# Linear attention with a butterfly FFN on one core: k^T (x | 1) in groups of 256 features, every key bank emptied by VectorE, and the whole last batch's attention output made by tokens

## What is computed

```python
q, k, v = split(x @ W_qkv)                      # 16 heads of 64 features each
q, k = relu(q @ W_f + b_f), relu(k @ W_f + b_f) # per head
kv = einsum('bhnd,bhne->bhde', k, v)
out = einsum('bhnd,bhde->bhne', q, kv)
out = out / (einsum('bhnd,bhd->bhn', q, k.sum(axis=2))[..., None] + 1e-06)
x = layernorm(x + merge_heads(out) @ W_out + b_out)
h = butterfly(x @ W_exp + b_exp, up_weights)    # 9 stages, 512 hidden features
h = butterfly(gelu(h + up_bias), down_weights)  # 9 stages
x = layernorm(x + h @ W_con + b_con + down_bias)
```

## Time and profile before

| | |
|---|---|
| median of three runs | 328.9 us |
| the profiled execution: time, span of its instructions | 328.99 us, 327.2 us |
| PE, PEld busy (share of the span) | 95%, 72% |
| DVE, ACT, POOL busy | 76%, 48%, 30% |
| chain that ended last, by engine | PE 76%, DVE 14%, issue 4%, ACT 2%, DMA 1%, POOL 1% |
| largest lines of that chain | ring L651 28%, kx_ps L738 14%, spare_ps L841 7%, attn_ps L651 7%, ring L758 4% |
| DMA queues | 33.95 MB, mean 104 GB/s |

### The profile page before, as it was taken

One profiled execution on the slowest core, in us unless ns is written; L12 is line 12 of the kernel. 1 busy time (PEld: TensorE's weight loads), 2 busy tenths in 40 slices (PEclk: granted clock), 3 DMA queues, 4 the chain that ended last, 5 costly groups with the idle time before them and its releaser, 6 DMA issues.

```text
span 327.2 us, 5512 instructions
## 1 busy us (share of the span) xinstructions
PE 311.2 (95%) x2009; PEld 234.4 (72%) x2009; DVE 249.9 (76%) x501; ACT 156.3 (48%) x279; POOL 97.1 (30%) x83
## 2 busy tenths in 40 slices
PE   5999999999999899999999999999999799999893
PEld 4766677767766677667768777776797587669793
DVE  3579989978989779888890997579838953758844
ACT  3634436535733343654461556346647846431442
POOL 4059999970000002400210122002302312423513
PEclk9999999999999989999999999999999999999998
DMA  4993425556705700370064002900190174372001
GB/s 140 311 327 128 134 75 184 189 201 148 175 2 136 151 0 2 103 160 0 5 156 105 0 35 68 195 0 32 20 229 16 36 167 94 93 159 75 1 34 64
DMA packets 19762, 33.95 MB, mean 104 GB/s; under 512 B 3960, under 2 KB 6680, under 8 KB 19736
## 3 DMA queue, kind: packets, MB, share of 16 engines
q1 hardware_dynamic: 19432, 33.54, 38.9%
q10 hardware_dynamic: 304, 0.07, 0.1%
HBM read 31.24 MB, written 2.36 MB: 103 GB/s over the span
## 4 chain that ended last, share of the span: by engine, by line
PE 76%; DVE 14%; issue 4%; ACT 2%; DMA 1%; POOL 1%; SPq 0%; POOLq 0%; DVEq 0%; ACTq 0%
PE ring L651 28%; PE kx_ps L738 14%; PE spare_ps L841 7%; PE attn_ps L651 7%; PE ring L758 4%; PE desk L772 3%; DVE qn L1335 2%; PE desk L660 2%; PE ring L718 2%; PE desk L747 2%; DVE k_total L1301 1%; DVE qn_l L1203 1%; DVE stats L1344 1%; DMA q<-in_L_attn_W_qkv_dram 1%; DVE k L1275 1%
## 5 line engine op out<-in xcount | busy, mean ns | idle before, releaser
L599 POOL TENSOR_TENSOR rstd<-var_eps,minus_half 128x4 f32<-128x4 f32 x14 | 19.3, 1381 | 176.9 <-DVE var_eps L1350 176.9
L1029 ACT ACTIVATE q<-ring,bf_col 128x512 f32<-128x512 f32 x64 | 43.9, 685 | 46.4 <-PE ring L651 45.6
L738 PE MATMUL kx_ps<-k,xs 128*128 128x512 f32 x128 | 60.3, 594 | 0.0
L1335 DVE TENSOR_TENSOR qn<-q,recips 128x512 f32<-128x512 f32 x64 | 43.5, 719 | 2.8 <-DMA recips<-recip_rows 2.8
L1013 ACT ACTIVATE qn_h<-qn 128x512 fp32r<-128x512 f32 x48 | 29.5, 625 | 27.5 <-DVE qn L1335 27.5
L582 POOL TENSOR_TENSOR y<-hid,y_up 128x512 f32<-128x512 f32 x18 | 32.8, 1843 | 15.9 <-DMA hid<-in_L_ffn_up_weights_dram 14.9
L738 PEld LDWEIGHTS kx_ps<-k,xs 128*128 128x128 f32 x128 | 24.2, 191 | 18.0 <-issue 15.4
L1301 DVE TENSOR_TENSOR k_total<-k_total,k 128x1024 f32<-128x1024 f32 x24 | 36.5, 1520 | 0.5 <-ACT k L1020 0.3
L1203 DVE TENSOR_TENSOR qn_l<-qn,qn_h 128x512 fp32r<-128x512 f32 x48 | 33.4, 704 | 2.9 <-ACT qn_h L1013 2.7
L651 PE MATMUL ring<-xT_h,wq_h 128*128 128x512 f32 x64 | 35.6, 556 | 0.0
L1275 DVE TENSOR_TENSOR k<-ring,bf_minus 128x512 f32<-128x512 f32 x32 | 21.9, 685 | 13.7 <-PE ring L651 13.7
(11 more groups left out here) (174 smaller groups left out, 580.6 us busy)
## 6 DMA issues: line engine op xcount, KB each, us to landing
recips<-recip_rows SPq DMA_DIRECT2D x64, 256.0 KB, 5.4
hid<-in_L_ffn_up_weights_dram SPq DMA_DIRECT2D x9, 512.0 KB, 4.2
x<-_L_ffn_down_weights_dram SPq DMA_DIRECT2D x9, 512.0 KB, 6.7
out_dram<-y SPq DMA_DIRECT2D x7, 256.0 KB, 2.0
xs<-in_L_attn_x_dram SPq DMA_DIRECT2D x3, 512.0 KB, 6.1
q<-in_L_attn_W_qkv_dram SPq DMA_DIRECT2D x2, 512.0 KB, 4.5
xs<-in_L_attn_x_dram SPq DMA_DIRECT2D x2, 256.0 KB, 2.7
q<-in_L_attn_W_qkv_dram SPq DMA_DIRECT2D x2, 256.0 KB, 3.9
```

The lines of the kernel that those rows point to most:

```text
L599: g.tensor_tensor(rstd[i][:, :], var_eps[i][:, :], minus_half[:, :].to_broadcast([128, QUADS]), ALU.pow).then_inc(s_rs[i], 1)
L738: t_.matmul(kx_ps[half], xs[b % XBUF][:, t, :], k[kt % KRING][:, half * CH:(half + 1) * CH], start=t == 0, stop=t == TILES - 1).then_inc(s ...
L1029: a_.activation(q[:, i % QRING, :], bank(("q", i))[:, :], ACT.Relu, bias=bf_col[:, :])\
L1335: v.tensor_tensor(qn[:, a % NRING, :], q[:, a % QRING, :], recips[:, a % PAIRS // RC, a % RC, :], ALU.mult).then_inc(s_qn, 1)
```

## The change

- **Key tiles by features.** A key tile is now 256 features (group g of a batch) by 512 tokens (chunk c). Each half of it holds 2 token tiles of 256 features side by side in a bank, so `project_k` makes six fp32r matmuls of 256 columns where it made three of 512.
- **All keys as max(z, -b).** The bias matmul, its rows and `k_relu` are gone; `k_max` on VectorE empties all 64 halves.
- **kx turned round.** `add_kx` takes the key (128 x 128) as weights and streams x with a column of ones behind it (129 columns), eight matmuls for a key tile, into one bank for each group. The last column is the sum of the keys, so `k_sum`, `k_total` and `ksum` are gone. ScalarE copies a group out (`kx_copy`), TensorE transposes it back (`transpose_kx`, eight 128 x 128 a batch, through `desk`), `kx_end` reads that by halves, and `ksum_mask` reads the sums from SBUF. xs has rows of 129 floats, the ones are written by GpSimd.
- **The start.** The first loads are x tiles 0 and 1, 256 columns of the k weights, x tiles 2 and 3; the other folds are spread over slots 0 to 4.
- **The butterflies.** Down stage 0 lies in slots 2 to 4, stages 1 to 8 in slots 5 to 12, one a slot, in two parts; `bias_row_step` is on GpSimd; the copies of wdn and vo are ScalarE's. Loads are reordered: up stages 4 and 5 and the last two batches of x go ahead of down stage 2, up 6 to 8 ahead of down 3, and `spread(0)` ahead of down 7.
- **The last batch by tokens.** Chunk 6 is made by tokens too; VectorE adds it to x straight from PSUM at the end of slot 38 (`add_x_before_last`), and the next chunk's first step waits for that. The bias b_out is added to the whole last batch of x by GpSimd.

The core of the diff:

```diff
@@ slots and tables
-    KX_SLOT = {TILES * b + FIRST + 1: b for b in range(BATCH)}
+    KXE_SLOT = {(TILES * b + 2 * g - 1 if b else g + 2): (b, g) for b in range(BATCH) for g in range(GROUPS)}
+    KXT_SLOT = {FIRST: (0, 0), FIRST + 2: (0, 1), TILES + FIRST: (1, 0), TILES + 6: (1, 1)}
+    for b in range(2, BATCH):
+        KXT_SLOT[TILES * b + 2] = (b, 0)
+        KXT_SLOT[TILES * b + 6] = (b, 1)
...
-    DOWN_STEP_SLOT = {1: 0, 2: 1, 3: 2, 5: 3, 6: 4, 7: 5, 8: 6, 9: 7, 12: 8}
+    DOWN_STEP_SLOT = {n + 4: n for n in range(1, STAGES)}
@@ SyncE
-            load_x(0, slice(0, 1), s_xs0)
-            for half in range(2):
-                cols = slice(HD + half * CH, HD + (half + 1) * CH)
-                sp.dma_start(wqkv_raw[:, cols], W_qkv[:, cols]).then_inc(s_wk[half], 16)
-            sp.wait_ge(s_wk[1], 16)
-            load_x(0, slice(1, 2), s_xs[0])
+            sp.dma_start(xs[0][:, 0:2, 0:C], xs_view[0, :, 0, 0:2, :]).then_inc(s_xs0[0], 16)
+            load_wk(0, slice(HD, HD + 256))
+            sp.dma_start(xs[0][:, 2:4, 0:C], xs_view[0, :, 0, 2:4, :]).then_inc(s_xs0[1], 16)
+            sp.wait_ge(s_wk[0], 16)
+            load_x(0, [1], s_xs[0])
+            load_wk(1, slice(HD + 256, HD + CH))
+            load_wk(2, slice(HD + CH, HD + 2 * CH))
...
+            load_down(3)
+            load_down(4)
             load_down(5)
             load_down(6)
+            spread(0)
             load_down(7)
-            spread(0)
             load_down(8)
@@ project_k
-                split(dst, (xT_h[:, b % 2, tok], xT_l[:, b % 2, tok]), (wk_h[:, cols], wk_l[:, cols]), stop=False)
-                t_.matmul(dst, ones_r[:, :], bf_rows[:, :], start=False, stop=True).then_inc(s_made, 1)
+                cols = slice(g * 256, (g + 1) * 256)
+                for i in range(2):
+                    t = QUADS * c + 2 * half + i
+                    tok = slice(t * 128, (t + 1) * 128)
+                    last = split(bank(("k", kt, half))[:, i * 256:(i + 1) * 256],
+                                 (xT_h[:, b % 2, tok], xT_l[:, b % 2, tok]), (wk_h[:, cols], wk_l[:, cols]))
+                last.then_inc(s_made, 1)
@@ add_kx
+                if c == 0 and GROUPS * b + g >= 2:
+                    pe.wait_ge(s_kxe, GROUPS * b + g - 1)
                 emptied(pe, ("k", kt, 1))
                 for half in range(2):
-                    t_.matmul(kx_ps[half], xs[b % XBUF][:, t, :], k[kt % KRING][:, half * CH:(half + 1) * CH],
-                              start=t == 0, stop=t == TILES - 1).then_inc(s_kxt, 1)
+                    for i in range(2):
+                        for j in range(2):
+                            col = half * CH + i * 256 + j * 128
+                            last = t_.matmul(kx_ps[g % 2][:, j * C1:(j + 1) * C1], k[kt % KRING][:, col:col + 128],
+                                             xs[b % XBUF][:, QUADS * c + 2 * half + i, :],
...
+            def transpose_kx(b, half):
+                take_desk(("kxT", b, half))
+                pe.wait_ge(s_kxe, GROUPS * b + 2 * half + 2)
+                transpose_tiles(desk, lambda i: kxT_pairs[:, 4 * half + i, 0:C]).then_inc(s_dmade, 1)
@@ add_attn
-                if a >= BATCH * STEPS - PAIRS:
+                elif a == PAIRS * LAST:
+                    pe.wait_ge(s_x1before, 1)
+                if a >= WHOLE:
@@ ScalarE
+            def kx_copy(b, g):
+                act.wait_ge(s_kxt, 2 * (TILES * b + 2 * (g + 1)))
+                if b:
+                    act.wait_ge(s_dmade, desk_of["kxT", b - 1, g // 2] + 1)
+                    act.wait_ge(s_kcols, b)
+                a_.activation(kxT[:, 2 * g * C1:2 * (g + 1) * C1], kx_ps[g % 2][:, 0:2 * C1], ACT.Copy).then_inc(s_kxe, 1)
@@ VectorE
             def ksum_mask(b):
-                dve.wait_ge(s_dmade, desk_of["ksum", b] + 1)
+                dve.wait_ge(s_kxe, GROUPS * (b + 1))
+            def add_x_before_last():
+                n = LAST - 1
+                at = n % CHUNKS * QUADS
+                dve.wait_ge(s_at, PAIRS * LAST)
+                dve.wait_ge(s_pre, n - X1BUF + 1)
+                dve.wait_ge(s_xb, 1)
+                v.tensor_tensor(x1[:, n % X1BUF, :, :], attn_ps[:, :].rearrange("p (t c) -> p t c", t=QUADS),
+                                xs[(BATCH - 1) % XBUF][:, at:at + QUADS, 0:C], ALU.add).then_inc(s_x1before, 1)
```

More of the change, by code:

```diff
@@ L192, in postln_linear_attention_butterfly_ffn_kernel @@
             order.append(("x", *XT_SLOT[s]))
-        if s == WDN_SLOT:
-            order.append(("wdn",))
+        if s == FIRST:
+            order.append(("vo", 3))
         if s in X1T_SLOT:
@@ L323, in postln_linear_attention_butterfly_ffn_kernel @@
         desk = pb("desk")
[L325 removed]
+        s_wk = [sem(f"k_weights_part_{n}_loaded") for n in range(3)]
         s_wq = sem("q_weights_loaded")
@@ L559, in _ @@
                             pattern=[[-1, 128]], channel_multiplier=1).then_inc(s_const, 1)
-            g.memset(ones_r[:, :].bitcast(fp32), 1.0)
-            g.memset(bf_rows[:, :].bitcast(fp32), 0.0).then_inc(s_bfz, 1)
-            g.memset(ones[:, :], 1.0)
+            for b in range(XBUF):
+                g.memset(xs[b][:, :, C:C1], 1.0).then_inc(s_xones, 1)
             g.memset(minus_half[:, :], -0.5)
@@ L609, in _ @@
                 up_step(n)
+            pool.wait_ge(s_up, 3 * STAGES)
+            for st in range(LOCAL):
+                bias_row_step(st)
             for s in range(SLOTS):
@@ L736, in add_kx @@
+                if c == 0 and GROUPS * b + g >= 2:
+                    pe.wait_ge(s_kxe, GROUPS * b + g - 1)
                 emptied(pe, ("k", kt, 1))
                 for half in range(2):
-                    t_.matmul(kx_ps[half], xs[b % XBUF][:, t, :], k[kt % KRING][:, half * CH:(half + 1) * CH],
-                              start=t == 0, stop=t == TILES - 1).then_inc(s_kxt, 1)
-            def ksum(b):
-                take_desk(("ksum", b))
-                if b == 0:
-                    pe.wait_ge(s_const, 3)
-                k_summed(pe, b, TILES - 1)
-                for p in range(PAIRS):
-                    last = t_.matmul(desk[:, p:p + 1], k_total[:, p * 128:(p + 1) * 128], ones[:, :],
-                                     start=True, stop=True)
-                last.then_inc(s_dmade, 1)
+                    for i in range(2):
[3 more added lines that the diff above has]
+                                             xs[b % XBUF][:, QUADS * c + 2 * half + i, :],
+                                             start=c == 0 and half == 0 and i == 0 and j == 0,
+                                             stop=c == 1 and half == 1 and i == 1 and j == 1)
+                    last.then_inc(s_kxt, 1)
@@ L1138, in _ @@
                 if s == 0:
[L1139 to L1145 removed]
+                    act.wait_ge(s_dmade, desk_of["x", 0, 1] + 1)
@@ new lines, in _ @@
+                if s == 1:
+                    act.wait_ge(s_dmade, desk_of["wq",] + 1)
+                    w_copy(0, 4, desk).then_inc(s_dtaken, 1)
+                    act.wait_ge(s_wT, 4)
+                    w_copy(4, 4, spare_ps).then_inc(s_wTa, 1)
+                    for half in range(2):
+                        act.wait_ge(s_fold, half + 4)
+                        hi(wq_h[:, half * CH:(half + 1) * CH], attn_ps[:, :], s_wh)
+                    act.wait_ge(s_dmade, desk_of["wcon",] + 1)
+                    a_.activation(y_dn_first, desk[:, :], ACT.Copy).then_inc(s_dtaken, 1)
```

594 lines of the change are left out of this document (292 added, 302 removed).

## The result

The changed kernel takes **325.43 us** (median of 4 runs, 324.97 to 327.18) against 329.0 for the kernel before in the same comparison: ratio 0.987, 95% interval 0.983 to 0.992. It is faster, by 3.6 us, where 8.4 were forecast. The profiled execution took 325.61 with a span of 323.8; before, 327.2. So the span lost 3.4. The 35 executions of the kernel before that ran beside the experiments took 327.5 to 331.9, the fastest with a mean granted clock of 1.00 and the slowest with 0.985 to 0.990, and its medians in the three comparisons there are 329.1, 329.7 and 331.2; so a difference of 1 to 2 us between two comparisons says little.

What follows compares the result with a forecast made beforehand. The prediction took TensorE's own work as the bound. Its terms, -7.8 - 3.2 - 0.7 + 0.3 + 2.5 + 0.5 = -8.4, took the profiled 328.99 us to 320.5 us, with a range of 315 to 326.

Steps and rivals of the forecast that it cites:

- the likeliest case: The whole kernel at 320.5 us, with its own range of 317.5 to 323.5 and a chance of 0.56.
- rival 2: Start at its upper bound, +3, and VectorE's lag in slots 10 to 12, +2: 325.5 us, chance 0.20.
- the start: Slot 0: new waits +2.75, smaller first loads -0.8, longer half pace +0.55; taken as +2.5 us.
- slot 30: GpSimd's bias addition doubles and slows a VectorE operation beside it: +0.3 us, bounds -2 and +1.
- the tail: PE's first step of chunk 7 waits for VectorE's add of chunk 6: +0.5 us, between 0 and 0.9.
- PE's work: Bias matmuls -7.4 and ksum -6.7 go; narrower kx +2.6, transposes +3.5 and small items come: sum -7.8 us.
- the place at 110 us: PE's wait for VectorE's copy of wdn goes, -1.5, and the clock loss behind it, -1.7: -3.2 us.
- two waits of the maps: Two of three PE waits in the maps for VectorE's add of x go: -0.7 us.
- rest of slots 1 to 12: VectorE's added evictions and down stages, and the reordered loads, stay covered there: taken at nothing.
- Rival 1: kx's weight loads are not hidden, 0.191 instead of 0.112 us for each of 512: +40, 361 us, chance 0.04.
- The signs: Trace marks: kx 0.112 us apart, no wait near slot 14, chunk 0's norm 3 us earlier, longest slot 0 wait before kx.
- The premise: The whole kernel is bound by TensorE's own work, so what the change takes from PE counts; bias matmuls -7.4 us.

Runs made afterwards that it cites:

- experiment 1: The changed kernel with stage 6 of the down weights moved out of the attention's bank: 322.93 us, ratio 0.980 to the kernel before.
- experiment 2: The changed kernel with the first recips spread ahead of stage 6's coefficients in SyncE's queue: 331.31 us, ratio 1.005 to the kernel before.
- experiment 3: The changed kernel with VectorE's sum over the first half of x moved earlier: 324.90 us, ratio 0.986 to the kernel before.
- experiment 6: The kernel of experiment 1 with 11 unused identity transposes filling PE's stops at the start: 322.58 us, ratio 0.980 to the kernel before.
- experiment 5: The kernel of experiment 1 with GpSimd's addition of b_out moved from slot 30 to slot 34: 321.59 us, ratio 0.976 to the kernel before.
- experiments 8 and 9: The kernel before without its 32 bias matmuls: 330.60 us, ratio 1.004; then also with two coefficient loads earlier in SyncE's queue: 326.39 us, ratio 0.989.

## Why the prediction was right and wrong

The sign, the range and the mechanism of the gain held; the forecast of the likeliest case was more than twice the gain. What came is rival 2 in its time (325.5), in its sense (relay and new waits cost more), but with another wait than the ones it names. That its time fits to 0.1 us is luck: it has +3 at the start and +2 in slots 10 to 12, measured were +1.5 and some +3.2, and slot 30 and the tail add the rest. One sum of the prediction is off: with the start at 0 the likeliest case's range begins at 318, not at 317.5.

| term | forecast | measured |
|---|---|---|
| PE's work | -7.8 | -8.1 by the chain's prices, -8.5 by PE's busy time |
| the place at 110 us | -3.2 | -3.4 (norm of chunk 1 to that of chunk 2: -4.4, of it 1.0 is work) |
| two waits of the maps | -0.7 | -0.7 (0.4 in one piece, where the earlier trace rows have 1.1 in three) |
| slot 30 | +0.3 | +0.9 (norm of chunk 6 to that of chunk 7) |
| start | +2.5 | +4.0 |
| rest of slots 1 to 12 | 0 | +3.0 to +3.4, of it 2.8 by experiment 1 |
| tail | +0.5 | some +1 |

- **PE's work: right.** kx takes 1.79 for eight matmuls, against 1.72 for the wide form, so 32 x 0.07 = +2.2 instead of 2.6; a key half 0.71 against 0.70; the rest as forecast. 129 columns with their own weights cost no more than 128. Rival 1 asked for 16 x 0.191 = 3.1 us for the eight; the row says 1.79, so in this fp32 form the loads are hidden. By the ratio that the prediction took from the Trainium skill, page "TensorE: Matmul & The Clock Gate", section "Back-to-back issue gap" (81 against 56 ns), it would be 16 x 0.162 = 2.6, an estimate that the 1.79 does not bear out.
- **110 us and the maps: right**, both the wait and the clock behind it.
- **The rest of slots 1 to 12, "at nothing": the step that failed**, with 2.8 us of the 5 that are missing (experiment 1; the wait in the row is 2.62, and 0.46 more stand ahead of a map at 83.76, where PE waits for VectorE's `m_l`). Three things in it were wrong. A stage was priced 3 x 0.7; it takes 1.10 + 1.10 + 0.69 = 2.9. The cover was sought in the key banks, and PE hardly waits for a key there; the bank that mattered is the attention's. And the move of the stages from slots 1 to 12 to slots 5 to 12 was costed as VectorE's work, not as a deadline: stage 6 was done 10.9 us ahead of the first attention product before, and now ends at 88.28, while PE is free at 85.8. The queue, on which the step also rests, is only in part to blame: VectorE waits 1.67 for recips, within the bound of 2, and PE hardly notices such a wait once the bank is free (experiment 1); while the bank was held, up to 1.7 of the stop hung on it (the estimate of experiment 2).
- **Start: the mechanism right, its size not.** Ahead of the first q product 17 bias matmuls are gone (-3.9), 7 kx groups and 17 key halves cost 0.7 more, and it starts 0.8 later: the start costs 4.0. The wait ahead of the first kx is near the 1.9 forecast (1.63 in the row; experiment 3 removes it), the first x comes 0.5 earlier instead of 0.8, and a wait of 0.46 for the k weights was not in the sum. The term that was mis-sized most is PE's pace, +0.55: half pace lasted until 11.7 us, where twelve key matmuls at 0.214 against 0.117 alone make 1.2, and with folds and transposes it is some 1.5 more than before. The profile's granted clock reads 1.00 there in both kernels, so the half pace is read from the distances alone. Why it lasts longer stays open: that PE stands more fits, but experiment 6 can't be told from the scatter.
- **Slot 30: the sign right, the rule read wrong.** The earlier trace rows were read as a VectorE operation slowed down; they show one that stands until GpSimd is done. Doubling the addition adds its whole 0.9 us to VectorE, and all that hangs on it in the stage is that late; taken away altogether it is worth 1.6 (experiment 5).
- **Tail.** The wait is 1.27 where 0.20 stood before, so 1.1 of the 1.3 worked out: the slack was some 0.2, not 0.4. The 0.4 for the transposes was counted twice, in PE's work and again here.
- **The signs.** kx at 0.112 an instruction, no wait and no clock fall near slot 14, and the longest wait of slot 0 ahead of the first kx: as said. The norm of chunk 0 starts 1.8 earlier, not 3, since slot 4 starts 0.8 later and not at the same time.
- **The premise**, that PE's saved work comes off the time, does not hold for the bias work alone: nothing of 7.4 us came off in the kernel before, and 3.4 with two loads earlier (experiments 8 and 9). The change also moves the stages later, and the x of batches 2 and 3 well ahead of stage 5's coefficients in the queue; the prediction named neither as needed for the gain, and no run tests which of the two the change needs.

## What to carry to other kernels

When a bound engine's work shrinks, look for the next thing that arrives by a clock of its own (a coefficient load paced by another engine, a scratch bank that is due at a certain slot) and write down how far ahead of its use it is now; a work item that is moved later gets a new deadline at every buffer that it holds, not only a new load on its engine. Try the removals together: two that were worth nothing alone (a filled stop, saved bias work) met another wait.
